# Fourth key chunk: rotation and splits on GpSimd, projections copied out by ScalarE

## The reference

```
x = x + 0.5 * ffn(layernorm(x))
x = x + attention(layernorm(x))
x = x + 0.5 * ffn(layernorm(x))
```

```
k = k * cos + rotate_half(k) * sin
```

## Time and profile before

| | |
|---|---|
| median of 3 runs | 752.54 us (752.45 to 753.93) |
| profiled execution | 753.2 us |
| its span in the trace | 751.4 us |
| mean granted TensorE clock | 0.967 |
| PE busy | 722.7 us (96%) |
| DVE busy | 690.1 us (92%) |
| ACT busy | 628.6 us (84%) |
| POOL busy | 277.6 us (37%) |

### The profile page before, as it was taken

How to read it: one execution, slowest core, us unless ns; L and a number is a source line. 1 busy time by engine, 2 the same in 40 slices (tenths; PEclk the granted TensorE clock), 3 DMA queues, 4 the chain that set the end, 5 groups by cost and what they waited for, 6 DMA issues and landing times.

```text
span 751.4 us, 17517 instructions
## 1 busy us (share of the span) xinstructions
PE 722.7 (96%) x6801; PEld 238.8 (32%) x6801; DVE 690.1 (92%) x876; ACT 628.6 (84%) x1190; POOL 277.6 (37%) x560
## 2 busy tenths in 40 slices
PE   5998989999999999999999999999999999999994
PEld 2763321222222222222222222222222222224383
DVE  6898899999999999999999999999999999996374
ACT  3554434999999999999999999999999999999842
POOL 4536334455454552333222222232233232424221
PEclk8997875999999999999999999999999999999998
DMA  7003110000011011110000000000000000000001
GB/s 225 5 1 78 34 48 1 5 5 25 14 26 36 18 23 33 23 34 13 4 4 4 4 5 4 20 3 5 3 5 4 5 7 20 8 6 5 6 15 42
DMA packets 25247, 15.51 MB, mean 21 GB/s; under 512 B 14134, under 2 KB 23158, under 8 KB 24902
## 3 DMA queue, kind: packets, MB, share of 16 engines
q1 hardware_dynamic: 12940, 10.84, 5.3%
q0 software_dynamic: 10016, 3.02, 2.2%
q10 hardware_dynamic: 2208, 0.53, 0.4%
HBM read 9.41 MB, written 3.31 MB: 17 GB/s over the span
## 4 chain that ended last, share of the span: by engine, by line
PE 80%; DVE 14%; issue 2%; ACT 1%; POOL 1%; DMA 1%; POOLq 0%; DVEq 0%; SPq 0%; ACTq 0%
PE ps L1388 33%; PE ps L1373 20%; PE ps L1352 13%; DVE mh L891 12%; PE ps L1228 4%; PE ps L1286 3%; PE ps L1303 2%; PE ps L1293 1%; PE ps L1324 1%; PE ps L1239 1%; PE ps L1403 1%; DMA X<-in_L_attn_x_dram 1%; PE ps L1217 1%; PE ps L1312 1%; PE ps L1413 0%
## 5 line engine op out<-in xcount | busy, mean ns | idle before, releaser
L891 DVE TENSOR_REDUCE mh<-ps 128x2 f32<-128x1024 f32 x512 | 586.6, 1212 | 10.5 <-PE ps L1352 9.9
L1185 ACT ACTIVATE ring<-ps 128x512 f32<-128x512 f32 x1024 | 550.3, 600 | 31.6 <-PE ps L1373 17.4
L1388 PE MATMUL ps<-ring,Vx 128*32 128x256 f32 x4096 | 325.8, 392 | 0.9 <-ACT outT L1193 0.9
L1373 PE MATMUL ps<-QT,KT 51*128 51x512 bf16 x1024 | 214.6, 389 | 1.1
L1352 PE MATMUL ps<-KT,QT 48*128 48x512 bf16 x1024 | 209.0, 389 | 2.7 <-ACT QT L1106 1.6
L1388 PEld LDWEIGHTS ps<-ring,Vx 128*32 128x32 f32 x4096 | 82.3, 108 | 187.2 <-ACT ring L1185 166.9
L1373 PEld LDWEIGHTS ps<-QT,KT 51*128 51x128 bf16 x1024 | 52.8, 93 | 220.2 <-ACT ring L1185 205.5
L630 POOL DMA_DIRECT2D rope<-outT x80 | 43.0, 542 | 185.8 <-ACT outT L1193 177.8
L619 POOL DMA_DIRECT2D QT<-mrow x128 | 71.3, 562 | 42.1 <-DVE mrow L908 37.5
L1352 PEld LDWEIGHTS ps<-KT,QT 48*128 48x128 bf16 x1024 | 50.6, 95 | 32.7 <-issue 14.3
L607 POOL TENSOR_TENSOR mp<-zeros,top 128x8 bf16<-128x8 f32 x32 | 6.4, 200 | 140.9 <-DVE top L899 140.8
(11 more groups left out here) (136 smaller groups left out, 371.1 us busy)
## 6 DMA issues: line engine op xcount, KB each, us to landing
rope<-rope_tables SPq DMA_DIRECT2D x2, 1024.0 KB, 6.7
QT<-mrow SPq DMA_DIRECT2D x128, 0.8 KB
QT<-mrow POOLq DMA_DIRECT2D x128, 0.8 KB, 1.7
rope<-outT POOLq DMA_DIRECT2D x80, 8.0 KB, 1.7
rope<-outT SPq DMA_DIRECT2D x80, 8.0 KB
q_bounce<-XB SPq DMA_DIRECT2D x3, 384.0 KB, 2.8
QT<-q_bounce SPq DMA_DIRECT2D x18, 64.0 KB
QT<-q_bounce POOLq DMA_DIRECT2D x18, 64.0 KB, 3.3
```

Of the source, the lines that this page charges most:

```text
L891: v.tensor_reduce(mh[:, g % 2, :, q, kb], ps[:, bank:bank + 2, :], AX.X, ALU.max)\
L1185: a.activation(ring[:, n % PRING, :], ps[:, exp_bank(n), :], ACT.Exp, scale=SCALE).then_inc(p_ready, 1)
L1373: t.matmul(ps[:, exp_bank(n), :], KT[rows, j, kt * P:(kt + 1) * P], QT[rows, j, c * CS:(c + 1) * CS], start=True, stop=True).then_inc(b_re ...
L1388: mm = t.matmul(ps[r:r + 32, PO, 0:QH], Vx[:, kt, col:col + 32], ring[:, (2 * n + h) % PRING, half * QH:(half + 1) * QH], start=(kt == 0), ...
```

## The change

The fourth key chunk K3 leaves VectorE. ScalarE copies its two projections with their bias into `turn` (`keep_k3`), behind `values(2)`. GpSimd multiplies by cosine and sine, adds, takes the rest and the last part, behind its `half_scatter(3)`; `value_bias(3)` moves in between. The two roundings of K3 stay on ScalarE where they were. VectorE's five K3 steps are gone. `KEPT_SEQ` counts ScalarE's copies in their new order.

```diff
+KEPT_SEQ = (("Q1", 0), ("Q1", 1), ("K3", 0), ("K3", 1), ("Q2", 0), ("Q2", 1), ("Q3", 0), ("Q3", 1))
...
-            if x in QK_SEQ:
-                return unit_turned, sum(y in QK_SEQ for y, _ in before)
-            return unit_kept, sum(y not in QK_SEQ for y, _ in before)
+            if x in QK_SEQ[:4]:
+                return unit_turned, sum(y in QK_SEQ[:4] for y, _ in before)
+            return unit_kept, KEPT_SEQ.index((x, k)) + 1
...
-                    pool.wait_ge(unit_kept, 2 * c)
+                    pool.wait_ge(unit_kept, KEPT_SEQ.index((f"Q{c}", 1)) + 1)
...
             value_bias(2)
+            half_scatter(3)
+            last = len(QK_SEQ) - 1
+            a, b = turn[:, last % 2, 0, :], turn[:, last % 2, 1, :]
+            cosine, sine = (rope[:, k, 3 * CS:4 * CS] for k in range(2))
+            pool.wait_ge(unit_kept, KEPT_SEQ.index(("K3", 0)) + 1)
+            g.tensor_tensor(a, a, cosine, ALU.mult).then_inc(k3_step, 1)
+            pool.wait_ge(unit_kept, KEPT_SEQ.index(("K3", 1)) + 1)
+            g.tensor_tensor(b, b, sine, ALU.mult).then_inc(k3_step, 1)
+            pool.wait_ge(k3_step, 2)
+            g.tensor_tensor(a, a, b, ALU.add).then_inc(whole, 1)
+            pool.wait_ge(cut0, last + 1)
+            g.tensor_tensor(b, a, parts[last % PARTS][:, 0, :], ALU.subtract).then_inc(rest_ready, 1)
             value_bias(3)
-            half_scatter(3)
+            pool.wait_ge(cut1, last + 1)
+            pool.wait_ge(cut2, last)
+            g.tensor_tensor(parts[last % PARTS][:, 2, :], b, parts[last % PARTS][:, 1, :], ALU.subtract).then_inc(cut2, 1)
             half_scatter(4)
...
                     rest("K2")
-                    turned_half("K3", 0)
-                if n == 8:
-                    turned_half("K3", 1)
                 if n == 9:
-                    turned_sum("K3")
                     last_part("K2")
-                if n == 12:
-                    rest("K3")
-                if n == 15:
-                    last_part("K3")
...
+            def keep_k3(k):
+
+                s = len(QK_SEQ) - 1
+                act.wait_ge(unit_ready, UNIT_SEQ.index(("K3", k)) + 1)
+                act.wait_ge(cut2, s - 1)
+                a.activation(turn[:, s % 2, k, :], ps[:, unit_bank("K3", k), :], ACT.Identity, bias=biasT[:, 1, k:k + 1])\
+                    .then_inc(unit_kept, 1)
...
             values(2)
+            keep_k3(0)
+            keep_k3(1)
             keep(2, 0)
             keep(2, 1)
             values(3)
```

More of the change, by code:

```diff
@@ L264, in macaron @@
         v_biased = sem("v_biased")
+        k3_step = sem("k3_step")
         half_out = [sem(f"half_out{s}") for s in range(len(QK_SEQ))]
```

## The result

The changed kernel takes 756.93 us (median of 5 runs, 756.86 to 758.62); the kernel before, in the same comparison, 752.45 (750.65 to 753.93). The ratio of the mean times is 1.0069 (95% interval 1.0047 to 1.0091): 5.2 us slower, 3.5 to 6.8. The medians lie 4.5 us apart. The profiled execution took 756.88 us with a span of 755.1. The forecast was 757.8, slower.

What follows compares the result with a forecast made beforehand. VectorE's 34 maxima before the exponentials were taken to bound the start of a loop without slack. Lateness of 3.9 to 6.6 us, middle 5.3, added to the median 752.5 gave 757.8 us; 80% range 754.5 to 759.8.

Steps and rivals of the forecast that it cites:

- GpSimd starts late: GpSimd's first K3 multiply, behind half_scatter(3)'s wait for K2's parts and six DMA issues, starts at about 94.5 us.
- The chain to the put of K2: From GpSimd's first K3 multiply at 94.5 to the end of ScalarE's put of K2 at 102.0: 7.5 us.
- The standstill: Before maximum 16, TensorE and VectorE wait for put K2, some 5.5 us.
- The clock: The standstill brings TensorE's clock down to 1.2 GHz sooner, so placements take 1.46 us instead of 0.82.
- my two figures: Lateness over maxima 16 to 23: 3.9 us if the clock stays high throughout, 6.6 us if low throughout.
- The loop gives nothing back: The attention loop, 18.3 us a group as before, recovers none of the time lost before it.
- What VectorE's relief is worth: Two K3 steps of 0.60 us leave VectorE's back-to-back reductions: 1.2 us gained if nothing else moved.
- Copies at no cost: ScalarE's two K3 copies of 0.69 us fall in its idle time between 85 and 87 us and cost nothing.
- Rival 1: Low clock ends early, maxima 24 to 33 run at 2.4 GHz, 3.8 us there: half won 754.5, 20%; all 752.6, 5%.

Runs made afterwards that it cites:

- e2: Changed kernel with GpSimd's half_scatter(3), which waits for K2's parts, moved behind its K3 steps: 750.32 us, ratio 0.9983 to the kernel before.
- e6: Changed kernel with two more 128 x 512 additions on GpSimd ahead of its K3 multiplies: 760.81 us, ratio 1.0125 to the kernel before.
- e1: Changed kernel with ScalarE's two cuts of K3 moved behind put K2 half 0: 755.69 us, ratio 1.0052 to the kernel before.
- e3: Changed kernel with 24 more dummy matmuls on TensorE between maxima 15 and 16: 756.23 us, ratio 1.0059 to the kernel before.
- changed again: Changed kernel rerun unchanged in another comparison: 759.18 us, ratio 1.0103 to the kernel before.
- e7: Kernel before with only ScalarE's copies of K3 added, VectorE doing the rest of K3 at its old places: 755.11 us, ratio 1.0040.
- e5: Changed kernel with half_scatter(3) behind GpSimd's K3 steps and K2's last part behind maximum 7, not 9: 751.64 us, ratio 0.9995 to the kernel before.
- e4: Kernel before with VectorE's five K3 steps cut to 8 of 512 columns: 751.45 us, ratio 0.9984.
- e8: Changed kernel, half_scatter(3) behind GpSimd's K3 steps, two dummies ahead of maxima 14 to 33: 748.01 us, ratio 0.9951 to the kernel before; again 749.01, 0.9965.
- e9: Kernel before with two dummy matmuls instead of one ahead of each maximum from 14 to 33: 749.28 us, ratio 0.9965.

## Why the prediction was right, step by step

To times of the trace after, 2.93 us are added where they are set against the trace before, since maximum 12 came that much earlier.

- **GpSimd starts late.** Foretold 94.5, measured 91.90 + 2.93 = 94.8. K2's last part ended when it should (88.7); SyncE's write and its landing took 2.59 us (85.79 to 88.38 on its queue) for the 2.56 foretold, and GpSimd woke 0.3 us after them.
- **The chain to the put of K2.** From the first multiply to the end of the put: foretold 7.5 us, measured 99.28 - 91.90 = 7.4.
- **The standstill.** Foretold some 5.5 us, measured 5.96 on PE and 5.68 on VectorE. e2 removes it by moving the wait, e6 lengthens it us for us, e1 shifts it to K3's own placement: shown, not only argued.
- **The clock.** At the lower level for maxima 16 to 23, so of my two figures the upper one applies: maximum 23 foretold 6.6 us late, measured 112.17 + 2.93 - 107.69 = 7.4. Of the 0.8 us between, 0.3 is GpSimd's waking; the rest is that maxima 16, 17 and 19 to 22 took 6.3 us on TensorE for my 5.9. I took the middle of 3.9 and 6.6 because the clock might return in the dense stretch. It did not return there in either trace of the changed kernel. The Trainium skill's rule that activity releases the throttle ("TensorE: Matmul & The Clock Gate", Part 1) came true only at 130 to 132 us, and at 132 to 134 in the second trace. e3 puts the clock's share at 2.9 us of 7.4. So the local loss of 7.4 us lies above my own 3.9 to 6.6, and the middle that I took, 5.3, was 2.1 us too small. That the first comparison gave 5.2 us is in part luck: its executions met a better clock elsewhere (2.9 us in the trace, ahead of maximum 12). The second comparison, 1.0103 or 7.7 us, shows the size. The first exponential's matmul, foretold near 125 us, ran at 124.29, and with the 2.93 added at 127.2: the same luck.
- **The loop gives nothing back.** 630.8 against 631.6 us: 0.8 us less. The higher clock came back about 6 us after the first exponential's matmul instead of 8. The six traces with one dummy and without the additional low stretch fit this: 630.6 to 630.8 us where it came back after 6 (changed, changed again, e7), 631.6 and 631.7 after 8 (before, e3), 632.9 after 11 (e1). The groups behind it are as foretold: VectorE is busy 18.30 us of 140.00 to 158.30 in both traces.
- **What VectorE's relief is worth.** Foretold 1.2 us if nothing else moved, and e5, where the clock fell at the same place as before, has 1.1 in the stretch. e2 and e4 have 2.4, with a later fall of the clock in them. Their medians are 1.9 and 0.8 us lower; no ratio of the three is clear of no change.
- **Copies at no cost.** Right where GpSimd reads them: they ran at 82.28 and 83.40, and maxima 9 to 12 keep their distances on TensorE. In e7, where VectorE reads them, it is wrong.
- **Rival 1, the low clock as a thing to win back.** It isn't what the change did, but the us were there: the medians of e8 and e9 are 3.0 to 3.6 us below the kernel before, of the 3.8 that I had counted.

## What to carry to other kernels

Before work is moved to an idle engine, look at what stands ahead of it in that engine's list, and not at its busy share: GpSimd was 37% busy, and ScalarE still waited 7.8 us for it, because a DMA wait and six issues stood in front. Then look who stands behind the consumer: here ScalarE's cut of K3 held back a copy of K2 that was ready. Independent work goes ahead of a wait, in both lists. And where TensorE only keeps pace with another engine, a second dummy matmul per step was worth 0.35%, clear of no change; the relief of that engine (e2, e4, e5) never was.

## What the hardware showed beyond that

- A VectorE operation with two inputs in SBUF beside a GpSimd one: 1.65 us instead of 0.68 in e2, ending 0.55 us after GpSimd's multiply (87.81 + 1.26 = 89.07); GpSimd's next one took 1.60 instead of 1.26. In e5, apart, 0.68 and 1.27. In e7 it is there again: VectorE's first multiply (82.88) took 1.27 us beside `value_bias(2)` on GpSimd (82.34 to 83.60) and ended 0.55 us after it; the second, alone, took 0.68. This adds about 0.6 us to what VectorE lost there. The Trainium skill ("SBUF — State Buffer", section "Who interferes with whom") calls the shared port pair an exclusive lock and says that the second to issue waits for the first. The numbers agree to 0.13 us: each of the two ended that much sooner than a full wait and its usual length would give. The maximum beside GpSimd's first multiply in e2, read from PSUM, took 1.23 us at 86.82, as the others do.
- Two additions of 128 x 512 on GpSimd that read one tile twice took 2.17 us together (e6), about 1.1 each. With two different float32 inputs one step takes 1.22 us from start to start (91.90 to 93.12).
- With one dummy ahead of each maximum the clock fell before the exponentials in all ten traces; with a second one from maximum 14 on it stayed at 1.00 through them and into the loop in all three.
